# A deformable-convolution block: bilinear coefficients are made on chip, one ScalarE pass and one VectorE sum per tap

## The reference

```python
out_normal = _conv(x, w_normal)
offset = concat([_conv(x, w_offx), _conv(x, w_offy)])      # 18 channels: dy, dx of 9 taps
out_x = _deform_conv(x, offset, w_dx)
out_y = _deform_conv(x, offset, w_dy)
out = _conv(concat([out_normal, out_x, out_y]), w_fusion)  # 384 -> 128
out = relu(_bn(out, bn1...))
out = _bn(_conv(out, w_conv2), bn2...)
return relu(out + x)

# _deform_conv, for each pixel and each of 9 taps: sample x at (py, px), then multiply by w
y0, x0 = floor(py), floor(px);  ty, tx = py - y0, px - x0
s = c(y0,x0)*(1-ty)*(1-tx) + c(y0,x0+1)*(1-ty)*tx + c(y0+1,x0)*ty*(1-tx) + c(y0+1,x0+1)*ty*tx
```

## Time and profile before

| | |
|---|---|
| median of 3 runs | 2737.15 us |
| profiled execution, span from first to last instruction | 2989.8 us |
| the profiled execution's own time | its span; the page gives nothing beside it |
| PE busy | 2685.1 us, 90% of the span |
| PEld busy | 2612.5 us, 87% |
| DVE busy | 1849.5 us, 62% |
| ACT busy | 2004.2 us, 67% |
| POOL busy | 1870.2 us, 63% |
| mean granted TensorE clock | 0.983 |
| bytes read from and written to HBM | 562.80 MB, 69.73 MB |

### The profile page before, as it was taken

How to read it: one execution, slowest core, us unless ns; L and a number is a source line. 1 busy time by engine, 2 the same in 40 slices (tenths; PEclk the granted TensorE clock), 3 DMA queues, 4 the chain that set the end, 5 groups by cost and what they waited for, 6 DMA issues and landing times.

```text
span 2989.8 us, 51480 instructions
## 1 busy us (share of the span) xinstructions
PE 2685.1 (90%) x17840; PEld 2612.5 (87%) x17840; DVE 1849.5 (62%) x4940; ACT 2004.2 (67%) x4925; POOL 1870.2 (63%) x1806
## 2 busy tenths in 40 slices
PE   1558899998999999999999999999999999999999
PEld 1458889998999998999899999999999999999999
DVE  3566666666666666666666666666666666666640
ACT  2566677776767676777677677776676776767741
POOL 3666666666666666666666666666666666666620
PEclk9789999999999999999999999999999999999999
DMA  9676667666666666666666767766666666666620
GB/s 278 202 231 193 206 200 220 202 208 198 205 205 201 198 208 199 201 206 205 204 204 203 215 209 219 215 181 186 183 186 183 181 182 186 186 182 185 179 90 23
DMA packets 218596, 579.32 MB, mean 194 GB/s; under 512 B 31840, under 2 KB 87264, under 8 KB 217952
## 3 DMA queue, kind: packets, MB, share of 16 engines
q0 software_dynamic: 144000, 471.97, 53.7%
q1 hardware_dynamic: 74336, 104.06, 10.5%
HBM read 562.80 MB, written 69.73 MB: 212 GB/s over the span
## 4 chain that ended last, share of the span: by engine, by line
PE 61%; ACT 13%; DVE 9%; issue 8%; another core or an unknown queue 7%; DMA 2%; POOL 1%; ACTq 0%; SPq 0%; POOLq 0%
PE work L363 13%; PE work L369 13%; PE work L366 13%; ACT mixed L495 5%; PE turned L395 5%; PE acc L369 5%; PE acc L366 5%; PE acc L363 5%; ACT samp L495 3%; DVE mixed L700 3%; PE work L348 2%; DVE feat L659 2%; DMA cell_table<-in_xpix 2%; DVE samp L706 2%
## 5 line engine op out<-in xcount | busy, mean ns | idle before, releaser
L318 POOL DMA_INDIRECT cells<-cell_table,index x1800 | 1859.0, 1033 | 1002.6 <-issue 390.4
L495 ACT ACTIVATE mixed<-cells,wgt 128x256 f32<-128x256 f32 x1800 | 758.0, 498 | 29.7 <-DMA cells<-cell_table,index 20.8
L495 ACT ACTIVATE samp<-mixed,wgt 128x128 f32<-128x128 f32 x1800 | 623.1, 396 | 205.6 <-issue 103.6
L700 DVE SCALAR_TENSOR_TENSOR mixed<-cells,wgt,mixed 128x256 f32<-128x256 f32 x1800 | 744.8, 478 | 21.8 <-ACT mixed L495 16.5
L363 PE MATMUL work<-feat,w_hi 128*128 128x320 f32 x2160 | 694.0, 321 | 13.7 <-issue 10.0
L369 PE MATMUL work<-feat,w_lo 128*128 128x320 f32 x2160 | 678.1, 314 | 10.9 <-issue 10.4
L366 PE MATMUL work<-feat,w_hi 128*128 128x320 f32 x2160 | 677.2, 314 | 7.4 <-issue 7.1
L706 DVE SCALAR_TENSOR_TENSOR samp<-mixed,wgt,samp 128x128 f32<-128x128 f32 x1800 | 512.0, 346 | 62.0 <-ACT samp L495 34.3
L659 DVE TENSOR_TENSOR samp_lo<-turned,samp_hi 128x640 fp32r<-128x640 f32 x360 | 295.8, 822 | 393.0 <-ACT samp_hi L494 329.2
L494 ACT ACTIVATE samp_hi<-turned 128x640 fp32r<-128x640 f32 x360 | 250.9, 697 | 374.3 <-remote 265.1
L363 PE MATMUL acc<-samp_hi,w_hi 128*128 128x320 f32 x1440 | 451.0, 313 | 11.9 <-issue 7.0
(11 more groups left out here) (70 smaller groups left out, 3199.4 us busy)
## 6 DMA issues: line engine op xcount, KB each, us to landing
cell_table<-in_xpix SPq DMA_DIRECT2D x54, 768.0 KB
cells<-cell_table,index POOLq DMA_INDIRECT x1800
x_raw<-in_xflat SPq DMA_DIRECT2D x40, 410.0 KB
cell_table<-in_xpix SPq DMA_DIRECT2D x2, 6912.0 KB, 38.3
late<-in_x SPq DMA_DIRECT2D x40, 320.0 KB
out<-late SPq DMA_DIRECT2D x40, 320.0 KB
late<-in_weights SPq DMA_DIRECT2D x3, 1152.0 KB, 32.5
cells<-in_weights SPq DMA_DIRECT2D x1, 657.0 KB, 4.1
```

Source lines behind the costliest of these rows:

```text
L318: eng.indirect_dma_start(out=cells[:, g, :], out_offset=None, in_=table[0:(b + 1) * CELLS, :], in_offset=bass.IndirectOffsetOnAxis(ap=inde ...
L495: return eng.activation(dst, src, ACT.Copy, scale=scale)
L700: eng.scalar_tensor_tensor(out=mixed[:, tp, j], in0=cells[:, (k * TILES + j) % GSLOTS, 2 * C:4 * C], scalar=wgt[:, par, 1, 0, j, k:k + 1], ...
```

## The change

Cells get another content. Of the corners a (upper left), b (upper right), c (lower left), d (lower right), the host now lays all four of a pixel position in one row of 512 numbers (`corners`, order a, b, c, d). On chip, VectorE makes coefficients of them: first b-a and d-c, then the lower pair minus the upper pair, so that the sample is (p + ty*q) + tx*(r + ty*s). SP loads a part of 384 cells (128 partitions of 3 cells) into the one buffer `coef`, VectorE does two subtractions, SP stores it into the table; 72 parts in all, 5 a step at first and 2 a step from step 9 to 26 (`PARTS_AT`). The strips of image 0 up to number 4 (`RAW`) are sampled in the old way, from `corners` itself; from strip 5 on the gathers read the table.

For strips from 5 on, a tile takes one multiply-add on VectorE over 256 columns straight from the cell (`rows_mixed`), then ScalarE multiplies the right half in place by tx (`weigh`), then VectorE adds the halves of all five tiles at once (`sampled`), in place. `samp` is gone, `mixed` has three buffers, `cells` 12 slots, and the pace lets gathers run 30 tiles ahead. VectorE's order in tap T is now `sampled(T+2)`, `samples_low(T+1)`, `rows_mixed(T+3)`, a part's coefficients, then the rest as before. In SP's step the parts come after the output's store, and the last weight chunk after them.

```diff
-PART = 768
+LOT = 3
+PART = 128 * LOT
 PARTS = CELLS // PART
+RAW = 5
+PARTS_AT = [5, 5, 4, 4] + [4, 4, 4, 3, 3] + 18 * [2]
+FIRST_PART = [sum(PARTS_AT[:i]) for i in range(len(PARTS_AT) + 1)]
-GSLOTS = 15
-PACE_LAG = 5 * TILES
+GSLOTS = 12
+PACE_LAG = 6 * TILES
+MIXED = 3
...
+        n = PARTS_AT[i] if i < len(PARTS_AT) else 0
+        self.parts = {j * TAPS // n: FIRST_PART[i] + j for j in range(n)}
...
-        mixed = sb("mixed", [128, 2, TILES, 2 * C])
-        samp = sb("samp", [128, 2, TILES, C])
+        coef = sb("coef", [128, LOT, 2, 2, C])
+        mixed = sb("mixed", [128, MIXED, TILES, 2 * C])
...
+            def load_part(p):
+                at_least(eng, part_out, 16 * p)
+                eng.dma_start(coef[...], part_rows(corners, p)).then_inc(part_in, 16)
+            def store_part(p):
+                at_least(eng, part_done, 2 * p + 2)
+                eng.dma_start(part_rows(table, p), coef[...]).then_inc(part_out, 16)
...
-            fill(0, CELLS, first_table)
             load_weights(1)
             load_x(1)
+            load_part(0)
             def step(i, par, fl):
                 if isinstance(i, int) and i == 0:
-                    eng.wait_ge(samp_done, PER // 3)
+                    eng.wait_ge(samp_done, 3)
...
                     load_weights(2)
-                    eng.wait_ge(w_lo_done, 3)
-                    load_weights(3)
...
-                if fl.table:
-                    at_least(eng, table_part, 32 * i)
-                    fill(CELLS + i * PART, PART, table_part)
                 if fl.second:
                     s = i - 4
                     at_least(eng, out_ready, 2 * s + 2)
                     eng.dma_start(out[:, bass.ds(s * PIX, PIX)], resid[:, par]).then_inc(out_stored[par], 16)
+                for p in fl.parts.values():
+                    store_part(p)
+                    if p + 1 < B * PARTS:
+                        load_part(p + 1)
+                if isinstance(i, int) and i == 1:
+                    eng.wait_ge(w_lo_done, 3)
+                    load_weights(3)
...
+            for c in range(NS):
+                b = c // STRIPS
+                if c < RAW:
+                    gather(c, c % 2, corners[0:CELLS, :])
+                    continue
+                if c == RAW or c % STRIPS == 0:
+                    eng.wait_ge(part_out, 16 * PARTS * (b + 1))
+                gather(c, c % 2, table[0:(b + 1) * CELLS, :])
...
+            def weigh(T):
+                if T >= TAPS * NS:
+                    return
+                k, par, raw = T % TAPS, T // TAPS % 2, T < TAPS * RAW
+                cols, side = (slice(0, C), 0) if raw else (slice(C, 2 * C), 1)
                 for j in range(TILES):
                     at_least(eng, mixed_done, TILES * T + j + 1)
-                    copy(samp[:, tp, j], mixed[:, tp, j, 0:C], scale=wgt[:, par, 0, 1, j, k:k + 1]).then_inc(left_done, 1)
+                    part = mixed[:, T % MIXED, j, cols]
+                    copy(part, part, scale=wgt[:, par, side, 1, j, k:k + 1]).then_inc(left_done, 1)
...
+            def rows_mixed(T):
+                if T >= TAPS * NS:
+                    return
+                k, par, raw = T % TAPS, T // TAPS % 2, T < TAPS * RAW
+                if not raw:
+                    at_least(eng, samp_turned, T - MIXED + 1)
                 for j in range(TILES):
+                    n = T * TILES + j
+                    cell, into = cells[:, n % GSLOTS, :], mixed[:, T % MIXED, j]
+                    if raw:
+                        at_least(eng, upper_done, n + 1)
+                    else:
+                        at_least(eng, cells_in[n % GSLOTS], 16 * (n // GSLOTS) + 16)
                     eng.scalar_tensor_tensor(
+                        out=into, in0=cell[:, 2 * C:4 * C], scalar=wgt[:, par, 1, 0, j, k:k + 1],
+                        in1=into if raw else cell[:, 0:2 * C], op0=ALU.mult, op1=ALU.add,
                     ).then_inc(mixed_done, 1)
+            def sampled(T):
+                k, par, buf = T % TAPS, T // TAPS % 2, T % MIXED
+                at_least(eng, left_done, TILES * T + TILES)
+                if T >= TAPS * RAW:
+                    ins = eng.tensor_tensor(mixed[:, buf, :, 0:C], mixed[:, buf, :, 0:C], mixed[:, buf, :, C:2 * C], ALU.add)
...
+            def coefficients(p):
+                at_least(eng, part_in, 16 * p + 16)
+                eng.tensor_tensor(coef[:, :, :, 1], coef[:, :, :, 1], coef[:, :, :, 0], ALU.subtract).then_inc(part_done, 1)
+                at_least(eng, part_done, 2 * p + 1)
+                eng.tensor_tensor(coef[:, :, 1], coef[:, :, 1], coef[:, :, 0], ALU.subtract).then_inc(part_done, 1)
...
+                    sampled(T + 2)
                     if fl.strip and (k < TAPS - 1 or fl.nxt):
                         samples_low(T + 1, 1 - tp)
+                    rows_mixed(T + 3)
+                    if k in fl.parts:
+                        coefficients(fl.parts[k])
...
-    xpix = np.ascontiguousarray(xflat.T)
+    xpix = xflat.T
+    corners = np.concatenate([xpix[o:o + B * CELLS] for o in (0, 1, PITCH, PITCH + 1)], axis=1)
```

More of the change, by code:

```diff
@@ L96, with __init__ @@
 class Flags:
-    def __init__(self, i=None, table=True):
+    def __init__(self, i=None):
         mid = i is None
@@ L132, in at_least, with deform_block @@
     eng.wait_ge(sem, value)
-def deform_block(nc, x, xflat, xpix, weights, bn, const, out):
+def deform_block(nc, x, xflat, corners, weights, bn, const, out):
     ctx = ExitStack()
@@ L248, in load_x, with part_rows @@
                 eng.dma_start(x_raw[:], xflat[:, bass.ds(start, SLOT)]).then_inc(x_in, 16)
[L250 to L255, removed]
+            def part_rows(of, p):
+                return of[p * PART:(p + 1) * PART, :].rearrange("(q n) c -> q (n c)", n=LOT)
+            def load_part(p):
+                at_least(eng, part_out, 16 * p)
+                eng.dma_start(coef[:, :, :, :, :].rearrange("q n a b c -> q (n a b c)"),
+                              part_rows(corners, p)).then_inc(part_in, 16)
+            def store_part(p):
+                at_least(eng, part_done, 2 * p + 2)
+                eng.dma_start(part_rows(table, p),
+                              coef[:, :, :, :, :].rearrange("q n a b c -> q (n a b c)")).then_inc(part_out, 16)
             def load_weights(n):
@@ L307, in _, with gather @@
             eng.memset(mid[:].bitcast(F32), 0.0).then_inc(zeroed, 1)
[L309 removed]
+            def gather(c, par, source):
                 at_least(eng, idx_ready, c + 1)
                 for q in range(PER):
[L312 to L317 removed]
+                    k, j, n = q // TILES, q % TILES, PER * c + q
+                    at_least(eng, mixed_done, n - GSLOTS + 1)
+                    at_least(eng, pace, n - PACE_LAG + 1)
                     eng.indirect_dma_start(
[L319 removed]
+                        out=cells[:, n % GSLOTS, :], out_offset=None, in_=source,
                         in_offset=bass.IndirectOffsetOnAxis(ap=index[:, par, j, k:k + 1], axis=0),
[L321 removed]
+                    ).then_inc(cells_in[n % GSLOTS], 16)
             eng.wait_ge(w_hi_done, 1)
             eng.wait_ge(w_lo_done, 1)
[L326 to L333 removed]
+            for c in range(NS):
[6 more added lines that the diff above has]
+                gather(c, c % 2, table[0:(b + 1) * CELLS, :])
         @block.tensor
@@ L416, in _ @@
             eng.wait_ge(w_lo_done, 2)
-            turn_samples(0, 0)
+            turn_samples(0)
             def step(i, par, fl):
@@ L552, in _ @@
             weights_high(1)
-            upper(0, 0, 0, 0, 0)
-            left(0, 0, 0, 0)
+            upper(0)
+            weigh(0)
             x_high(1, 1)
-            upper(1, 0, 1, 0, 1)
+            upper(1)
+            upper(2)
             samples_high(0, 0)
-            left(1, 1, 0, 1)
-            upper(2, 0, 2, 0, 0)
+            weigh(1)
+            upper(3)
             eng.wait_ge(bn_step, BN_STEPS)
@@ L566, in step @@
                     tp = (par + k) % 2
-                    if fl.strip and k < TAPS - 2:
-                        left(T + 2, k + 2, par, tp)
-                    elif fl.strip and fl.nxt:
-                        left(T + 2, k + 2 - TAPS, 1 - par, tp)
+                    weigh(T + 2)
                     if fl.strip and (k < TAPS - 1 or fl.nxt):
@@ L574, in step @@
                         weights_high(fl.weights[k])
-                    if fl.strip and k < TAPS - 3:
-                        upper(T + 3, i, k + 3, par, 1 - tp)
-                    elif fl.strip and fl.nxt:
-                        upper(T + 3, i + 1, k + 3 - TAPS, 1 - par, 1 - tp)
+                    upper(T + 4)
                     if k == fl.turn and fl.nxt:
@@ L756, in _ @@
             weights_low(1)
-            sample(0, 0, 0, 0)
+            rows_mixed(0)
+            sampled(0)
             x_low(1, 1)
-            sample(1, 1, 0, 1)
+            rows_mixed(1)
+            rows_mixed(2)
             samples_low(0, 0)
```

(1 more changed line is left out.)

72 lines of the change are left out of this document (27 added, 45 removed).

## The result

The changed kernel takes 2822.83 us (median of 4 runs, 2817.32 to 2824.81) against 2737.99 us of the kernel before on the same chip (4 runs): a ratio of 1.0303, with a 95% interval of 1.0288 to 1.0317. It is 84.8 us slower; 29 us faster had been forecast.

What follows compares the result with a forecast made beforehand. It took PE's instructions to bound the kernel from step 2 on. Terms of -29, -10, +7 and +3 summed to -29 us, from the median 2737.15 to 2708 us; range 2635 to 2760, the forecast's own 2690 to 2733.

Steps and rivals of the forecast that it cites:

- The start: Before the first transposes: gathering from the host's corners ends the wait for the table, -29 us (bounds -29 and -20).
- ScalarE and VectorE per tap: Strips from 5 on: less work per tap shortens PE's waits for samples, -10 us (bounds 0 and -28).
- sum of floors: Whole kernel before: PE's instruction times without gaps, plus start and tail, sum to 2744 us, near the median 2737.15.
- The coefficients: Making 72 parts on VectorE: +7 us over steps 0 and 1 from 12 us round trips; nothing in steps 9 to 26.
- SyncE's order: Steps 4 to 6: parts queued behind the output store stall VectorE, 1 us a step, +3 us (bounds 0 and 15).
- Its own sign of being wrong: The prediction would be wrong if, among other signs, steps 0 to 3 took over 275 us together.
- The other signs: Expected in the profile: ScalarE busy about 1350 us, VectorE near 1800, subtractions near 0.96 us.
- Slots and pace: Gathers: 12 slots give 15 us of lead instead of 18.8, no starvation seen, 0 us (bounds 0 and +10).
- The round trip decides: Rival, chance 0.14: with one buffer, 18 us load-and-store trips stall VectorE in steps 0 to 3; 2780 us.
- cancelling: Rival, chance 0.14: a part's round trip of 15 us takes back 28 of the 29 us gained; no change, 2737 us.
- A faster PE: Rival, chance 0.22: without the profiler PE's work is 59 us of a 64 us step, the rest shortenable waits; 2623 us.

Runs made afterwards that it cites:

- e4: Changed kernel with the new sampling in all 40 strips, gathering plain host corners as if coefficients, no coefficients made; 2712.69 us.
- e0: Kernel before, unchanged, profiled a second time; span 2738.8 us, run 2740.61 us.
- e1: Kernel before with every gather reading the host's corners, the table and its fills gone; 2705.59 us, ratio 0.9878.
- e2: Changed kernel with the coefficient parts of steps 7 to 26 moved to later taps (4 and 6; 2, 4, 6 in steps 7 and 8); 2778.68 us.
- e8: Changed kernel with each coefficient part at its tap, but behind that tap's convolution outputs in VectorE's order; 2780.32 us.
- e7: Changed kernel with all part transfers, waits and places, but each subtraction over one column per corner instead of 128; 2753.10 us.
- e5: Kernel before with all gathers from the host's corners and 12 cell slots in place of 15, old order of taps; 2706.17 us.
- e6: Changed kernel with all strips on the raw path, no parts, and 15 cell slots instead of 12; 2766.49 us.
- e3: Changed kernel with all 40 strips on the raw path of strips 0 to 4, no parts or table, 12 slots; 2800.25 us.

## Why the prediction was wrong

Where the 80.8 us between the two spans lie: -27.3 the start, +45.5 steps 0 to 4, +51.5 the parts from step 5 on (10.6 + 40.9, against e4), +11.1 the new order from step 5 on (e4 against e0).

**The start, -29: right.** 27.3 us in the profile, and e1 shows that this part of the change does it alone.

**ScalarE and VectorE per tap, -10: wrong by all of it.** Its waits were read from an execution 253 us longer than any run. The prediction's own sum of floors had landed on the median and said that from step 2 on the runs were bound by PE; its lower bound, 0, was the one to take. That sum met the median partly by luck: in e0 steps 0 and 1 are 9 us shorter than in it, steps 2 to 4 8 us longer; the 34 steps after them are as it had them. e0 has no PE wait in those steps, and e4 no gain.

**The coefficients, +7: the step that failed.** "From step 9 to 26 there are two parts a step, 3.8 us, against 9 x 0.6 = 5.4 saved; nothing shows." It weighed VectorE's time as an amount. The saved 0.6 us lie in every tap, and the part stands whole in tap 0, ahead of the second convolution's output, which PE waits for (703.23 above). Against the same sampling without parts (e4) it cost 40.9 us in steps 9 to 26 (1207.2 - 1166.3) and 10.6 in 5 to 8, some 2.5 of which are SyncE's order (below). e2 and e8 remove 40.9 and 41.0 of the former by place alone. The subtraction itself was priced well; groups of instructions in the kernel after (busy us, mean ns | idle before), for the earlier trace rows:

```profile
L737 DVE TENSOR_TENSOR mixed<-mixed 128x640 f32<-128x640 f32 x315 | 260.1, 826 | 406.1 <-ACT mixed L508 405.0
...
L750 DVE TENSOR_TENSOR coef<-coef 128x768 f32<-128x768 f32 x72 | 69.0, 958 | 2.5
L748 DVE TENSOR_TENSOR coef<-coef 128x768 f32<-128x768 f32 x72 | 68.7, 955 | 33.5 <-DMA coef<-in_corners 33.4
```

The idle column of L737 tells the same: VectorE sat 405 us before its sums, waiting for ScalarE. That is room for 138 us of parts, if they stand there.

**The same term in steps 0 to 4.** Only the round trip was priced, by VectorE's stalls. Page of the kernel after, DMA issues (KB each, median us from issue to landing), for the earlier trace rows:

```profile
coef<-in_corners SPq DMA_DIRECT2D x72, 768.0 KB, 6.6
coef_table<-coef SPq DMA_DIRECT2D x72, 768.0 KB, 4.6
```

With 1.9 us of subtractions that is 13.1 us, near the 12 taken, and VectorE waited for parts for 15.8 us in these steps. e7, which has the trips and the waits, costs 7.6 us for them. The 24.8 beside it are VectorE's own time, in steps where samples are late and PE waits for them; the prediction counted VectorE as covered there. Its own sign of being wrong came: steps 0 to 3 took 294.7 us together, over its 275. The other signs came as forecast: ScalarE busy 1396.8 us, VectorE 1793.7, subtractions of 0.96 us.

**SyncE's order, +3: right, by the trace.** The stall stands where it was forecast, at the second part of steps 4, 5 and 6: VectorE waits 5.09, 6.48 and 5.38 us there, and PE's next transposes start 0.41, 1.78 and 0.67 us late, 2.9 in all. SP, DVE and PE in the kernel after, step 5:

```profile
433.97 0.34 SPq L302 DMA_DIRECT2D out<-late  x1
434.36 0.43 SPq L268 DMA_DIRECT2D coef_table<-coef  x1
...
446.80 0.96 DVE L748 TENSOR_TENSOR coef<-coef 128x768 f32<-128x768 f32 x1 [6.48 <-DMA coef<-in_corners]
...
450.37 0.74 PE L408 MATMUL turned<-cst,mixed 128*128 128x128 f32 x5 [1.78 <-DVE samp_lo L674]
```

The part's store goes out right behind the output's, though its subtractions were done before 427 us. No run isolates the term.

**Slots and pace, 0: right for the slots alone (e5), wrong for the change.** (The two gathers that the forecast quotes for 1.25 us lie 1.32 apart; 1.25 is the distance of the later ones.) The order of taps came with them, and no term stood for it: on the raw path 5 us in steps 0 to 4 with 15 slots, 20 with 12, and 0.33 us in each later step of the new sampling. The account of steps 0 to 4, from e1 on: 320.7, order 325.8 (e6), with 12 slots 340.8 (e3), the parts' trips 348.4 (e7), VectorE's subtractions 373.2. These are one path from e1 to the changed kernel; as e5 shows, the same edit costs otherwise in another place.

**The rivals.** The round trip decides, 2780 us, had the right side by the wrong mechanism: trips of 13 us, not 18, and time lost mostly elsewhere; cancelling, too, asked for trips of 15. A faster PE is excluded by e0: busy throughout at 64.47 us a step. The warm gap of the Trainium skill that the prediction weighed ("TensorE: Matmul & The Clock Gate", section "Back-to-back issue gap") would give a step of about 59 us, an estimate; the page calls it the gap of isolated matmuls, and here a weight load stands before each. The trace doesn't agree, with 64.47.

## What to carry to other kernels

Where the bound engine is busy without a gap, ask of each added instruction not whether its engine has time but what stands behind it in that engine's list and who waits for that; in steps 9 to 26 the same 1.9 us cost nothing one place further back. Take a stall for real only if the profiled execution takes as long as the runs, and try the part of a change that needs no other part by itself: here the host's corners alone are 1.2% faster than before, and everything built upon them lost.

## What the runs showed of the hardware

TensorE's clock made small waits dearer where PE is the bound. In steps 9 to 26 of the kernel after, the granted clock fell from 1.00 to 0.50 (from 2.4 to 1.2 GHz) for 3.4 us five times; in e0 it did so not once between 400 and 2500 us. Windows around the first of them, in step 15:

```profile
1080.60:1105.20 24.60, 22.91 (x158) 22.41 (x157) 16.55 (x31) 11.06 (x28) 15.82 (x16) 1.00 0.65 189
1105.20:1108.60 3.40, 3.40 (x14) 3.40 (x15) 2.03 (x4) 3.25 (x10) 1.81 (x2) 0.50 0.97 375
1108.60:1148.80 40.20, 40.20 (x280) 40.16 (x280) 25.45 (x57) 18.16 (x44) 28.78 (x29) 1.00 0.78 254
```

Just before, PE had waited 1.41 us for the output and 0.28 for `off_c`, as in every step there; the five steps with the fall took 68.15 us, the others 66.65, so 7.5 us in all, about the 7 by which e2 beat its expectation. Why the clock fell in these five steps and not in the other thirteen, the runs do not show.

In steps 0 to 4 a lower clock did not set the time. The mean granted clock there is 0.90 in e1, 0.89 in e3 and 0.85 in the kernel after, which looks like a part of the price. But e2 runs the same instructions in these steps as the kernel after. Windows of e2, steps 0 to 4:

```profile
38.85:412.10 373.25, 273.69 (x1652) 264.32 (x1653) 264.31 (x645) 239.43 (x584) 253.45 (x232) 0.88 0.79 268
```

Half-clock time is twice the missing share times the length: 112 us in the kernel after (2 x 0.15 x 373.25) and 90 in e2 (2 x 0.12 x 373.25). With 22 us less of it, e2 takes the same 373.25 us. These steps wait for samples, and the slower matmuls seem to fall into time in which PE would have waited.
